# Window attention: scores on four 64x64 tiles into two banks, weighted sums with loaded values in column tiles, norms transposed back into their own bank

## The chip, the cores and the metric

The kernel runs on one core of one Trainium2 chip, as one program in which the instructions of every engine are written out by hand. TensorE is called PE here, VectorE DVE, ScalarE ACT, GpSimd POOL and SyncE SP. The metric is the time of one execution in device microseconds (us). Three executions of the kernel before took 2562.41 us (median), 2558.15 and 2567.25 us.

## The reference

The input `x` is (8, 128, 64, 64). It goes through a block of window attention and then through a binarized 3x3 convolution with a batch norm.

```python
WIN, HEADS, DOWN, STRIDE = 8, 8, 4, 2            # 64 tokens in a window, 8 heads of 16 channels
def mha(q, k, v, wq, wk, wv, wf, bf):
    qh, kh, vh = (q @ wq), (k @ wk), (v @ wv)    # each split into 8 heads of 16
    attn = softmax(einsum('bqhd,bkhd->bhqk', qh, kh) / sqrt(16))
    return einsum('bhqk,bkhd->bqhd', attn, vh) @ wf + bf

# level 0: self attention in 8x8 windows of x, layernorm; averaged 4x4 -> a 16x16 map
# level 1: the same on the 16x16 map -> kv
# cross:   q = 8x8 windows of level 0; k, v = 8x8 windows of kv, two pixels apart
q = layernorm(level0 + mha(level0_windows, kv_windows, kv_windows, ca_wq, ...))
out = layernorm(q + relu(q @ ffn_w1 + b1) @ ffn_w2 + b2)
y = conv3x3(sign(out), sign(weight)); result = out + batchnorm(y)
```

Each window has, for each of its 8 heads, a 64x64 matrix of scores, its softmax, and a weighted sum of 64 values of 16 channels.

## The kernel before

**Units and pairs.** An image is cut into 8 strips of 8 rows; a strip has 8 windows of 64 tokens, taken two at a time: four pairs. The unit of work is one strip of self attention (64 `self` units), one strip of cross attention with the feed-forward part and a strip of the convolution (64 `cross` units), or the 16x16 map of an image (8 `low` units of two pairs). That makes 528 pairs. The first 16 self units run alone; then self and cross units take turns, 96 units of 4 pairs each, with a low unit put in here and there; the last 16 cross units run alone. After them comes a tail that applies the batch norm and adds (DMA, ACT and DVE; PE has no work there).

**What sets the order.** `stages_in_order` gives every stage of a unit an offset in pairs (the tables `SELF`, `CROSS`, `LOW`, `LAST_CONV`), sorts all stages of all units by unit start plus offset, and every engine issues its own stages in that one order. Pair `k` of a unit has `rough` at `k - 1.95`, `scores` at `k - 1.0`, `exp` at `k - 0.98`, `prob_lo` at `k - 0.96` and `weigh` at `k + 0.5`. So, in the time of one pair, PE meets in this order: the scores of pair n, the rough scores of pair n+1, whatever has an offset whose fraction lies between 0.05 and 0.5, the weighted sum of pair n-1, and whatever has a fraction from 0.5 to 1. I call the two places for other work the **first gap** (rough to weigh) and the **second gap** (weigh to the next scores and rough). DVE has the reduction of the rough scores (`maxima`) at the `rough` place and `normalise` at the `weigh` place.

**One pair.** `rough_scores` (L591) makes the 8 heads x 2 windows of 64x64 scores into `ps_max`, window w on partitions 64w to 64w+63. DVE reduces them (L897, `negmax`). `scores` (L601) makes them again, transposed, into `ps_s`, and L607 subtracts the maxima by 16 small matmuls. ACT takes the exponential twice (L769 in f32, L770 in f16) and POOL the difference (L1055). `weigh` (L620) is 12 matmuls with the probabilities loaded (128x128) and 68 columns of values streamed, into `ps_o`; column 32 of a block of values is one, so that the sum of the probabilities comes out beside them. `normalise` takes the reciprocal of the 8 sums a token (L904) and multiplies (L909, twice) into `onorm`, which has tokens on its partitions.

**One unit.** `turn` (L633) transposes `onorm` on PE into `ps_t`, ACT copies it to `oT` (L781, four pieces), and `project` (L652) multiplies by `wf` into `ps_y`, onto which `resid` (L639, L641) had put the input and the bias. `stats` (L919, L924), `rstd` on POOL and `apply` (L932) normalise; `spread` (L660) transposes back into `ps_t`; ACT applies gain and shift (L801). A cross unit then has `h0` to `h3` (L672), `f0` to `f3` (L683), a second norm (L938, L943, L951), `out` (L691) into `ps_t`, and `conv` (L702). The projections of q, k and v go through `ps_proj` (L535, L560); v is split into two f16 parts (L748 on ACT, L880 on DVE) and moved into the windowed layout `vb` by a DMA (`move_v`). For cross units the values come from DRAM (`fetch_v`).

Each of `ps_proj, ps_hid, ps_max, ps_s, ps_o, ps_t, ps_y, ps_y2` is one bank of PSUM. `rough` waits for the reduction of the pair before (`s_neg`), `weigh` for the normalise of the pair before (`s_on`): the two chains don't touch one another.

## Time and profile before

| | |
|---|---|
| three executions | 2562.41 us median (2558.15 to 2567.25) |
| the profiled execution | 2557.35 us, of which the span of the trace is 2555.5 us |
| PE busy | 2160.4 us (85%) |
| DVE busy | 1596.3 us (62%) |
| ACT busy | 1368.0 us (54%) |
| POOL busy | 943.8 us (37%) |
| mean granted PE clock | 0.937 of full speed |
| tail after the last pair | about 165 us without PE work |

The page counts an engine as busy from the start to the end of an instruction's row. On PE these rows overlap heavily, since a row includes the time in which results run out of the array; the distance between the starts of two blocks of matmuls is what a block costs PE. The chain that ended last is followed back from the last instruction, always to what released it.

### The profile page before, as it was taken

The page shows a single profiled execution, that of the slowest core. Times are in us where ns is not written, and L with a number is a line of the kernel's source. Part 1 is how long each engine was busy: PE and PEld are TensorE (multiplying, and loading weights), DVE is VectorE, ACT ScalarE, POOL GpSimd, SP SyncE. Part 2 cuts the span into 40 slices and gives each one's busy share as a digit, 9 for nine tenths or more (in the row PEclk, how much of TensorE's full clock was granted, in tenths as well). Part 3 has the DMA queues.
Part 4 walks back from the last instruction along what each step waited for, and adds up shares of the span by engine and source line. Part 5 has one row for each costly group of instructions (what it writes and reads, how often), then busy time and mean ns, then how long its engine had stood idle before and what let it go on. Part 6 is the DMA issues. An engine that isn't in the chain of part 4 may idle for free.

```text
span 2555.5 us, 93135 instructions
## 1 busy us (share of the span) xinstructions
PE 2160.4 (85%) x39704; PEld 1729.7 (68%) x39704; DVE 1596.3 (62%) x5098; ACT 1368.0 (54%) x2531; POOL 943.8 (37%) x1080
## 2 busy tenths in 40 slices
PE   6987889997999979998899979999799989898700
PEld 4776767775777757776677757777677767676400
DVE  4886766676666757776576656676567655555332
ACT  3664555664556646665455645565456544555332
POOL 3443443443344334434344433443344433333100
PEclk9999999999999989998899989999899999999955
DMA  6775655554555545554455545555455544432177
GB/s 183 210 196 162 190 147 160 168 164 125 155 165 166 154 122 165 164 158 137 132 166 151 166 120 151 160 168 143 129 162 162 161 120 118 122 113 85 44 238 261
DMA packets 335102, 393.57 MB, mean 154 GB/s; under 512 B 40033, under 2 KB 239458, under 8 KB 334690
## 3 DMA queue, kind: packets, MB, share of 16 engines
q1 hardware_dynamic: 333842, 386.62, 52.5%
q8 instruction: 315, 5.16, 0.9%
q10 hardware_dynamic: 848, 0.99, 0.1%
q14 instruction: 97, 0.79, 0.1%
HBM read 208.29 MB, written 160.27 MB: 144 GB/s over the span
## 4 chain that ended last, share of the span: by engine, by line
PE 58%; DVE 28%; DMA 4%; ACT 4%; issue 4%; POOL 1%; SPq 0%; POOLq 0%; DVEq 0%; ACTq 0%
PE ps_hid L672 9%; PE ps_y L683 9%; PE ps_proj L535 6%; PE ps_o L620 6%; DVE onorm L909 5%; PE ps_s L601 4%; PE ps_hid L702 3%; PE ps_s L607 3%; PE ps_t L633 3%; DVE negmax L897 3%; DVE xn L951 3%; PE ps_max L591 3%; PE ps_y L652 2%; PE ps_y L639 2%; DVE xn L932 2%
## 5 line engine op out<-in xcount | busy, mean ns | idle before, releaser
L1055 POOL TENSOR_TENSOR prob_lo<-prob,prob_hi 128x512 f16<-128x512 f32 x528 | 611.1, 1157 | 913.9 <-ACT prob_hi L770 913.9
L769 ACT ACTIVATE prob<-ps_s 128x512 f32<-128x512 f32 x528 | 313.6, 594 | 399.8 <-PE ps_s L607 394.1
L897 DVE TENSOR_REDUCE negmax<-ps_max 128x8 bf16<-128x512 f32 x528 | 360.4, 683 | 119.8 <-PE ps_max L591 115.5
L904 DVE RECIPROCAL rden<-ps_o 128x8 f32<-128x8 f32 x528 | 107.1, 203 | 518.7 <-PE ps_o L620 517.8
L909 DVE TENSOR_TENSOR onorm<-ps_o,rden 64x128 f32<-64x128 f32 x1056 | 304.9, 289 | 25.5
L770 ACT ACTIVATE prob_hi<-ps_s 128x512 f16<-128x512 f32 x528 | 313.5, 594 | 0.0
L620 PE MATMUL ps_o<-vb,prob_hi 128*128 128x68 f16 x4224 | 293.8, 197 | 3.1 <-DVE onorm L909 2.9
L672 PE MATMUL ps_hid<-xf,w_sb 128*128 128x512 f32 x512 | 286.0, 641 | 3.0 <-ACT yconv L827 2.1
L683 PEld LDWEIGHTS ps_y<-w_sb,hid 128*128 128x128 f32 x2048 | 266.5, 196 | 31.7 <-issue 26.8
L683 PE MATMUL ps_y<-w_sb,hid 128*128 128x128 f32 x2048 | 277.6, 280 | 0.6 <-ACT hid L808 0.6
L620 PEld LDWEIGHTS ps_o<-vb,prob_hi 128*128 128x128 f16 x4224 | 260.7, 100 | 9.7 <-issue 5.4
L620 PE MATMUL ps_o<-vb,prob_lo 128*128 128x68 f16 x2112 | 259.1, 197 | 0.0
L1046 POOL TENSOR_TENSOR vareps<-mv,consts_sb 128x4 f32<-128x4 f32 (+1 forms) x200 | 39.7, 198 | 536.8 <-DVE mv L924 305.2
L601 PE MATMUL ps_s<-qs,ks 64*64 64x64 f16 x8448 | 235.2, 197 | 1.5 <-ACT prob_hi L770 1.5
L601 PEld LDWEIGHTS ps_s<-qs,ks 64*64 64x64 f16 x8448 | 176.2, 110 | 81.8 <-issue 55.1
L607 PE MATMUL ps_s<-identb,negmax 64*64 64x64 bf16 x8448 | 225.0, 195 | 3.8 <-DVE negmax L897 3.8
L591 PE MATMUL ps_max<-ks,qs 64*64 64x64 f16 x8448 | 225.3, 195 | 0.2 <-issue 0.2
L620 PEld LDWEIGHTS ps_o<-vb,prob_lo 128*128 128x128 f16 x2112 | 204.5, 100 | 23.5 <-issue 4.1
L781 ACT ACTIVATE oT<-ps_t 64x256 f32<-64x256 f32 (+1 forms) x544 | 201.6, 371 | 14.5 <-PE ps_t L633 7.8
L808 ACT ACTIVATE hid<-ps_hid,columns_sb 128x512 f32<-128x512 f32 x256 | 175.9, 687 | 57.9 <-PE ps_hid L672 55.8
L1049 POOL TENSOR_TENSOR rstd<-vareps,consts_sb 128x4 f32<-128x4 f32 (+1 forms) x200 | 198.8, 994 | 15.7
L932 DVE TENSOR_SCALAR xn<-ps_y,mv,rstd 128x128 f32<-128x128 f32 x528 | 180.3, 403 | 27.8 <-POOL rstd L1049 26.8
(106 smaller groups left out, 3554.0 us busy)
## 6 DMA issues: line engine op xcount, KB each, us to landing
k_rows<-k_flat SPq DMA_DIRECT2D x256, 256.0 KB, 3.2
qs<-q_rows SPq DMA_DIRECT2D x512, 128.0 KB, 3.2
ks<-k_rows SPq DMA_DIRECT2D x128, 512.0 KB, 4.9
q_rows<-q_flat SPq DMA_DIRECT2D x128, 256.0 KB, 2.4
vb<-v_flat SPq DMA_DIRECT2D x128, 136.0 KB, 4.2
vb<-values_out SPq DMA_DIRECT2D x128, 136.0 KB, 2.9
xin<-in_x SPq DMA_DIRECT2D x64, 256.0 KB, 3.1
self_out<-xa SPq DMA_DIRECT2D x64, 256.0 KB, 3.6
```

Source lines behind the costliest of these rows:

```text
L591: done = mm(ps_max[r, TOK * h:TOK * h + TOK], qs[u.b][r, h, k, :], ks[u.b][r, h, k, :], start=True, stop=True, skip_group_check=True)
L601: mm(ps_s[r, TOK * h:TOK * h + TOK], ks[u.b][r, h, k, :], qs[u.b][r, h, k, :], start=(h == 0), stop=False, skip_group_check=True)
L607: done = mm(ps_s[r, TOK * h:TOK * h + TOK], negmax[r, pair_no(u, k) % 2, h:h + 1].to_broadcast([64, TOK]), identb[r, r], start=False, stop ...
L620: done = mm(ps_o[:, 2 * VC * j:2 * VC * j + 2 * VC].rearrange("p (w c) -> p w c", w=2), pp[:, pair_no(u, k) % 2, 128 * j:128 * j + 128], v ...
L672: mm(ps_hid[:, :], w1_sb[:, C * b:C * b + C], xf[:, u.no % 2, :], start=True, stop=True, skip_group_check=True).then_inc(s_hid, 1)
L683: done = mm(ps_y2[:, C * p:C * p + C], hid[:, b % 2, C * p:C * p + C], w2_sb[:, b, :], start=False, stop=(b == FB - 1), skip_group_check=True)
L769: activation(prob[:, pair_no(u, k) % 2, :], ps_s[:, :], ACT.Exp)
L770: activation(prob_hi[:, pair_no(u, k) % 2, :], ps_s[:, :], ACT.Exp).then_inc(s_exp, 1)
L897: v.tensor_reduce(negmax[:, pair_no(u, k) % 2, :], ps_max[:, :].rearrange("p (a t) -> p a t", t=TOK), AX.X, ALU.max, negate=True).then_inc ...
L909: done = v.tensor_tensor(onorm[r, u.seq % 2, k, :].rearrange("p (w j d) -> p j w d", w=2, j=4), blocks[r, :, :, DH * h2:DH * h2 + DH], r2[ ...
L932: v.tensor_scalar(xn[:, C * p:C * p + C], ps_y[:, C * p:C * p + C], mv[:, p, 0:1], rstd[:, p:p + 1], ALU.subtract, ALU.mult).then_inc(s_xn, 1)
L1055: g.tensor_tensor(prob_lo[:, i, :], prob[:, i, :], prob_hi[:, i, :], ALU.subtract).then_inc(s_prob, 1)
```

## The change

1. **Scores.** In `rough_scores` and `scores` even heads now write partitions 0 to 63 and odd heads 64 to 127, window 0 into the first and window 1 into the second of two banks (`ps_max` and `ps_s` are two banks each, 256 columns used in each). The 16 matmuls of 64x64 so fall on four row and column positions of the array, where they fell on two. The matmuls that subtract the maxima load a 128-row, 64-column operand.
2. **Weighted sums.** `weigh` now loads values (128 rows x 32 columns) and streams probabilities: 24 matmuls of 64 columns into `ps_o`, and 8 of 128 columns with a loaded block of ones (`vone`) into `ps_sum`, on four column positions. The result has channels on its partitions, and every channel has its own copy of the sum. `ps_o` and `ps_sum` are columns 256 to 511 of the first bank of `ps_max`; hence `max_free`: a rough block waits for the normalise of the weigh block before it, and a weigh block for the reduction of the rough block before it.
3. **Normalise** takes a reciprocal of 128x128 and one product of 128x128, straight into `oT`. `turn`, `turned`, `onorm` and `ps_t` are gone; `project` waits for the last normalise.
4. **Transposes back.** `spread` writes into `ps_y` and `out` into `ps_y2`, over what they were made from. `resid` waits for `s_spread_taken` and `resid2` for `s_out_taken`, where they waited for `s_xn` and `s_xn2`.
5. **Values.** `project_v` is 16 matmuls of 64x64 (f32) into both halves of the partitions, `v_hi` and `v_lo` are two instructions each on 64 partitions and write `vb` directly; `move_v` is gone. `VC` is 32, and the blocks that `fetch_v` brings are zero in half of their channels: 64 x 2048 f16 for each DMA, 64 x 1088 before.
6. All offsets are new.

```diff
-VC = 34
+VC = 2 * DH
...
-SELF = dict(load=-10.6, q=-7.8, q_hi=-7.6, q_lo=-7.45, q_put=-7.3, q_move=-5.7, k=-6.8, k_hi=-6.6, k_lo=-6.45,
-            k_put=-6.4, k_move=-5.1, v=-5.8, v_hi=-5.6, v_lo=-5.45, v_move=-4.3, turn=4.16, turned=4.24, resid=5.2,
...
+SELF = dict(load=-11.6, q=-7.8, q_hi=-7.6, q_lo=-7.45, q_put=-7.3, q_move=-5.7, k=-6.8, k_hi=-6.6, k_lo=-6.45,
+            k_put=-6.4, k_move=-5.1, v=-4.65, v_hi=-4.4, v_lo=-4.2, resid=4.0, project=4.4, stats=4.6, rstd=4.65,
+            apply=5.15, spread=5.86, spread_out=5.96, store=6.4, pool=6.9)
...
+    max_use, use = {}, None
+    for stage, u, what in order:
+        if stage in ("rough", "weigh"):
+            max_use[stage, u.seq, what] = use
+            use = (stage, pair_no(u, what))
...
-        ps_proj, ps_hid, ps_max, ps_s, ps_o, ps_t, ps_y, ps_y2 = (
-            bank(n) for n in ("ps_proj", "ps_hid", "ps_max", "ps_s", "ps_o", "ps_t", "ps_y", "ps_y2"))
+        ps_max, ps_s = two_banks("ps_max"), two_banks("ps_s")
+        ps_proj, ps_hid, ps_y, ps_y2 = (bank(n) for n in ("ps_proj", "ps_hid", "ps_y", "ps_y2"))
+        ps_o, ps_sum = ps_max[:, 0, 256:384], ps_max[:, 0, 384:512]
...
+            def max_free(stage, u, k):
+                if max_use[stage, u.seq, k] is not None:
+                    before, no = max_use[stage, u.seq, k]
+                    pe.wait_ge(s_neg if before == "rough" else s_on, no)
...
             def rough_scores(u, k):
...
-                if pair_no(u, k) > 1:
-                    pe.wait_ge(s_neg, pair_no(u, k) - 1)
+                max_free("rough", u, k)
                 for h in range(HEADS):
+                    to, at = slice(64 * (h % 2), 64 * (h % 2) + 64), TOK * (h // 2)
                     for win in range(2):
                         r = slice(64 * win, 64 * win + 64)
-                        done = mm(ps_max[r, TOK * h:TOK * h + TOK], qs[u.b][r, h, k, :], ks[u.b][r, h, k, :],
+                        done = mm(ps_max[to, win, at:at + TOK], qs[u.b][r, h, k, :], ks[u.b][r, h, k, :],
                                   start=True, stop=True, skip_group_check=True)
...
-                        r = slice(64 * win, 64 * win + 64)
-                        done = mm(ps_s[r, TOK * h:TOK * h + TOK],
-                                  negmax[r, pair_no(u, k) % 2, h:h + 1].to_broadcast([64, TOK]),
-                                  identb[r, r], start=False, stop=True, skip_group_check=True)
+                        n = 4 * win + h // 2
+                        done = mm(ps_s[to, win, at:at + TOK],
+                                  negmax[:, pair_no(u, k) % 2, n:n + 1].to_broadcast([128, TOK]),
+                                  identb[:, to], start=False, stop=True, skip_group_check=True)
...
             def weigh(u, k):
...
                 pe.wait_ge(s_prob, pair_no(u, k))
-                if pair_no(u, k) > 1:
-                    pe.wait_ge(s_on, pair_no(u, k) - 1)
-                for j in range(4):
+                max_free("weigh", u, k)
+                i = pair_no(u, k) % 2
+                for win in range(2):
                     for n, (pp, part) in enumerate(((prob_hi, 0), (prob_lo, 0), (prob_hi, 1))):
-                        done = mm(ps_o[:, 2 * VC * j:2 * VC * j + 2 * VC].rearrange("p (w c) -> p w c", w=2),
-                                  pp[:, pair_no(u, k) % 2, 128 * j:128 * j + 128], vb[u.b][:, :, part, 4 * k + j, :],
-                                  start=(j == 0 and n == 0), stop=(n == 2), skip_group_check=True)
+                        for j in range(HEADS // 2):
+                            at = 256 * win + TOK * j
+                            mm(ps_o[VC * j:VC * j + VC, TOK * win:TOK * win + TOK], vb[u.b][:, part, k, win, j, :],
+                               pp[:, i, at:at + TOK], start=(win == 0 and n == 0), stop=(n == 2),
+                               skip_group_check=True)
+                for n, pp in enumerate((prob_hi, prob_lo)):
+                    for j in range(HEADS // 2):
+                        done = mm(ps_sum[VC * j:VC * j + VC, :].rearrange("p (w t) -> p w t", w=2), vone[:, :],
+                                  pp[:, i, :].rearrange("p (w j t) -> p j w t", w=2, t=TOK)[:, j, :, :],
+                                  start=False, stop=(n == 1), skip_group_check=True)
                 done.then_inc(s_pv, 1)
...
             def attention_residual(u):
                 if before_resid[u.seq] is not None:
-                    pe.wait_ge(s_xn, xn_done[before_resid[u.seq].seq])
+                    pe.wait_ge(s_spread_taken, spread_no["spread", before_resid[u.seq].seq, None])
...
             def project_out(u):
-                pe.wait_ge(s_t_taken, turn_no["turn", u.seq, None])
+                pe.wait_ge(s_on, last_pair(u))
...
-                v.reciprocal(r2, blocks[:, :, :, 32]).then_inc(s_rden, 1)
+                v.reciprocal(rden[:, i, :], ps_sum).then_inc(s_rden, 1)
                 dve.wait_ge(s_rden, pair_no(u, k))
-                for h2 in range(2):
-                    r = slice(64 * h2, 64 * h2 + 64)
-                    done = v.tensor_tensor(
-                        onorm[r, u.seq % 2, k, :].rearrange("p (w j d) -> p j w d", w=2, j=4),
-                        blocks[r, :, :, DH * h2:DH * h2 + DH],
-                        r2[r, :, :].unsqueeze(3).to_broadcast([64, 4, 2, DH]), ALU.mult)
-                done.then_inc(s_on, 1)
+                v.tensor_tensor(oT[:, u.seq % 2, C * k:C * k + C], ps_o, rden[:, i, :], ALU.mult).then_inc(s_on, 1)
```

In the names of the rows below, `[waits ...]` are the semaphores that an instruction waits for. On PE in the middle of the program, before, at the place where a cross unit's q projection stands: `consts_sb,onorm` is the turn, `w_sb,hid` the feed-forward part.

```order
L591 MATMUL ps_max<-ks,qs 64x64 [waits s_neg]
L591 MATMUL ps_max<-ks,qs 64x64 x15
L633 MATMUL ps_t<-consts_sb,onorm 128x128 [waits s_t_taken,s_on]
L633 MATMUL ps_t<-consts_sb,onorm 128x128 x3
L683 MATMUL ps_y<-w_sb,hid 128x128 [waits s_hid_taken]
L683 MATMUL ps_y<-w_sb,hid 128x128 x3
L535 MATMUL ps_proj<-xin,wq_sb 128x256 [waits s_proj_lo,s_xin0]
L535 MATMUL ps_proj<-xin,wq_sb 128x256
L620 MATMUL ps_o<-vb,prob_hi 128x68 [waits s_on,s_prob,s_v_moved0]
```

The same place of the program with the change: between a rough block and the weigh block stand a q projection, both parts of the second residual, a feed-forward part, a hidden block and the output projection of a self unit.

```order
L597 MATMUL ps_max<-ks,qs 64x64 [waits s_on]
L597 MATMUL ps_max<-ks,qs 64x64 x15
L531 MATMUL ps_proj<-xin,wq_sb 128x256 [waits s_proj_lo,s_xin1]
L531 MATMUL ps_proj<-xin,wq_sb 128x256
L647 MATMUL ps_y<-consts_sb,xf 128x128 [waits s_out_taken]
L647 MATMUL ps_y<-consts_sb,xf 128x128 x3
L649 MATMUL ps_y<-brow,ones 128x512
L691 MATMUL ps_y<-w_sb,hid 128x128 [waits s_hid_taken]
L691 MATMUL ps_y<-w_sb,hid 128x128 x3
L680 MATMUL ps_hid<-xf,w_sb 128x512 [waits s_hid_taken]
L660 MATMUL ps_y<-wf_sb,oT 128x128 [waits s_on]
L660 MATMUL ps_y<-wf_sb,oT 128x128 x3
```

The rough block waits for `s_on` where it waited for `s_neg`, and the turn is gone. What stands in the first gap is now unequal from pair to pair: in this pair it is the most, in two of eight pairs nothing.

On DVE, before, around one `normalise` (L904, L909) and the reduction (L897):

```order
L904 RECIPROCAL rden<-ps_o 128x8 [waits s_pv]
L909 TENSOR_TENSOR onorm<-ps_o,rden 64x4x2x16 [waits s_rden]
L909 TENSOR_TENSOR onorm<-ps_o,rden 64x4x2x16
L867 SCALAR_TENSOR_TENSOR q_flat<-ps_proj,q_flat 128x2x256 [waits s_proj_hi]
L938 BN_STATS stats<-ps_y 128x6 [waits s_f]
```

With the change (`ps_max` stands here for `ps_o` and `ps_sum`, which lie in it):

```order
L917 RECIPROCAL rden<-ps_max 128x128 [waits s_pv]
L920 TENSOR_TENSOR oT<-ps_max,rden 128x128 [waits s_rden]
L870 SCALAR_TENSOR_TENSOR q_flat<-ps_proj,q_flat 128x2x256 [waits s_proj_hi]
L965 TENSOR_REDUCE colsum<-xa 128x128 [waits s_pooled,s_spread_taken]
L971 TENSOR_REDUCE low_sum<-colsum 128x32 [waits s_xlow,s_colsum]
```

The reciprocal grew from 8 to 128 elements on each partition, and two products became one.

## Rows read from the trace of the kernel before

**Rows 1.** The page: busy time by engine, and the chain that ended last.

```profile
PE 2160.4 (85%) x39704; PEld 1729.7 (68%) x39704; DVE 1596.3 (62%) x5098; ACT 1368.0 (54%) x2531; POOL 943.8 (37%) x1080
...
PE 58%; DVE 28%; DMA 4%; ACT 4%; issue 4%; POOL 1%; SPq 0%; POOLq 0%; DVEq 0%; ACTq 0%
```

**Rows 2.** Stretches, instructions on `rden` (three a pair): busy, PEclk, DMA share, GB/s.

```profile
40.00:260.00 220.00, 48.51 (x189) 0.98 0.69 192
600.00:1800.00 1200.00, 208.43 (x801) 0.95 0.53 151
2040.00:2380.00 340.00, 47.12 (x181) 0.96 0.37 107
```

**Rows 3.** Who waited for whom: us in total, times, longest.

```profile
DVE rden L904 <- PE ps_o L620: 517.8, 285, 4.3
...
PE ps_t L633 <- DVE onorm L909: 9.3, 31, 1.1
...
PE ps_o L620 <- DVE onorm L909: 2.9, 12, 1.0
```

**Rows 4.** Groups by line and shape: busy us, mean ns | idle before, releaser.

```profile
L897 DVE TENSOR_REDUCE negmax<-ps_max 128x8 bf16<-128x512 f32 x528 | 360.4, 683 | 119.8 <-PE ps_max L591 115.5
...
L909 DVE TENSOR_TENSOR onorm<-ps_o,rden 64x128 f32<-64x128 f32 x1056 | 304.9, 289 | 25.5
...
L781 ACT ACTIVATE oT<-ps_t 64x256 f32<-64x256 f32 x512 | 193.0, 377 | 11.4 <-PE ps_t L633 4.9
...
L904 DVE RECIPROCAL rden<-ps_o 128x8 f32<-128x8 f32 x528 | 107.1, 203 | 518.7 <-PE ps_o L620 517.8
```

**Rows 5.** PE in order of time at full clock: start, length, instructions.

```profile
1247.52 0.60 PE L639 MATMUL ps_y<-consts_sb,xin 128*128 128x128 f32 x4
...
1248.17 0.60 PE L639 MATMUL ps_y<-consts_sb,xf 128*128 128x128 f32 x4
...
1249.71 0.19 PE L620 MATMUL ps_o<-vb,prob_hi 128*128 128x68 f16 x1
...
1250.05 0.20 PE L620 MATMUL ps_o<-vb,prob_hi 128*128 128x68 f16 x1
1250.18 0.44 PE L601 MATMUL ps_s<-qs,ks 64*64 64x64 f16 x16
1250.45 0.42 PE L607 MATMUL ps_s<-identb,negmax 64*64 64x64 bf16 x16
...
1250.70 0.42 PE L591 MATMUL ps_max<-ks,qs 64*64 64x64 f16 x16
1251.05 1.12 PE L672 MATMUL ps_hid<-xf,w_sb 128*128 128x512 f32 x2
1252.02 1.05 PE L652 MATMUL ps_y<-wf_sb,oT 128*128 128x128 f32 x8
...
1258.96 0.63 PE L633 MATMUL ps_t<-consts_sb,onorm 128*128 128x128 f32 x4
1259.43 1.06 PE L683 MATMUL ps_y<-w_sb,hid 128*128 128x128 f32 x8
1260.32 1.03 PE L535 MATMUL ps_proj<-xin,wq_sb 128*128 128x256 f32 x4
...
1270.25 2.12 PE L702 MATMUL ps_hid<-smap,convs 128*128 128x512 bf16 x9
1272.31 0.44 PE L601 MATMUL ps_s<-qs,ks 64*64 64x64 f16 x16
```

**Rows 6.** DVE in order of time, the same stretch.

```profile
1250.29 0.21 DVE L904 RECIPROCAL rden<-ps_o 128x8 f32<-128x8 f32 x1 [2.35 <-PE ps_o L620]
...
1253.11 0.89 DVE L919 BATCH_NORM_STATS2 stats<-ps_y 128x6 f32<-128x128 f32 x4 [1.25 <-PE ps_y L652]
...
1255.88 1.37 DVE L932 TENSOR_SCALAR xn<-ps_y,mv,rstd 128x128 f32<-128x128 f32 x4 [0.68 <-POOL rstd L1049]
...
1258.92 0.69 DVE L897 TENSOR_REDUCE negmax<-ps_max 128x8 bf16<-128x512 f32 x1 [0.33 <-PE ps_max L591]
```

262 lines of the change are left out of this document (123 added, 139 removed).

## The prediction

> **What bounds the kernel now.** I read the busy shares first [rows 1]: PE 85%, DVE 62%, ACT 54%, POOL 37%, so PE is the fullest engine, but the chain that ended last is PE for only 58% and DVE for 28%. A kernel bound by PE alone would show PE throughout. Then the pace [rows 2]: with three `rden` instructions a pair, 63 pairs take 220 us where self units run alone (3.49 us a pair), 267 take 1200 us in the middle (4.49), 60.3 take 340 us where cross units run alone (5.64). The clock there is 0.95 to 0.98, so it stands at its lower level (1.2 GHz) for a few per cent only. Third, the waits [rows 3]: DVE waited 517.8 us for weighted sums, which is slack of DVE; a weigh block waited 2.9 us for the normalise before it, the turn 9.3 us. Last, a stretch in order of time [rows 5, 6] shows the period: scores, maxima, rough scores, other work, weighted sum. At full clock a block costs PE the distance to the next start: scores 0.27, maxima 0.25, rough 0.35, weigh 0.47, together 1.34 us a pair.
>
> **What PE loses and gains in a pair.** The 16 matmuls of a score block take 0.25 us on two positions of the array [rows 5]. On four positions they take 0.13 if these really work at once; that is worth 2 x 0.12. The maxima block keeps two positions: 0.25. The weigh block has 12 matmuls in 0.34 + 0.03 us. The new one streams 24 x 64 and 8 x 128 columns in four column positions; at the 0.03 us that 68 columns take now this is 40 times 0.03 over four, 0.29 us (at two positions' spacing of 15 ns each, 0.48). So 0.3 us are saved. Against this stands a change of shape: inside a weigh block starts are 0.03 apart, from its last one to the scores 0.13, and rough to the next work is 0.35 where maxima to rough is 0.25 [rows 5]. A change of tile shape costs 0.09 to 0.1. There are two a pair now; with 64x64, 128x64, 64x64, 128x128, 128x32 and 128x128 there are four to six. They cost 0.2 to 0.4 us. PE gains nothing in a pair. The Trainium skill (TensorEngine Tiling (Array Packing), Key Properties) says that changing the tiling mode drains the engine; that speaks against this change, and the trace's 0.1 us agrees.
>
> In a unit PE loses the turn, 0.47 us [rows 5], 136 times: 64 us less. ACT loses four copies of 377 ns, 1.5 us a unit [rows 4]. The values' projection keeps its column passes on two positions at best, and gets two changes of shape; ACT and DVE each get one more instruction of some 0.6 us in a self unit. The DMA that moved values goes; the fetched block grows from 1088 to 2048 elements a row. DMA engines are at 0.53 [rows 2], and the fetch stands over four pairs ahead of its use: nothing.
>
> **Normalise.** Products of 128 elements take 289 ns, a reduction of 512 elements 683 ns [rows 4]: 1.03 ns an element and a fixed 150 to 157 ns. The reciprocal takes 203 ns for 8 elements. Either its fixed part is 195 ns, and 128 elements take 0.33 us; or its fixed part is that of the others and each element takes (203 - 152)/8 = 6.4 ns, and 128 take 0.97 us. No other DVE row here has a fixed part as large as 195, so I take 0.97 and keep 0.33 as the other end. With the product (0.35 with its hand-over) normalise is then 1.32 us (or 0.68); now it is 0.203 and two products, 0.8 us and the hand-over [rows 4]. The Trainium skill (VectorE: DVE Perf Modes, Walkthrough: the 8-slice pipeline in each mode) describes the reciprocal as an iterative division with a repeat count of 8; taken as 8 cycles an element it would lie near the slow end, but the page gives no duration.
>
> **The shared bank.** This is the largest term. With the change rough waits for the normalise of the weigh ahead of it, and weigh for the reduction of the rough ahead of it; what stands behind either on PE's queue waits too. One turn of this loop is: hand-over 0.05, weigh 0.30 at the clock of the middle, 0.23 until DVE starts (0.58 from first start to normalise now, less 0.34), normalise R + 0.35, hand-over 0.05, rough 0.13, 0.20 until DVE starts (the row of 0.42 less 0.25, and 0.03), reduction 0.71. That is 2.02 + R: 2.99 us, or 2.35. Other work comes on top as far as it doesn't fit in the gaps: in the first gap PE has about 0.8 us while DVE reduces, DVE 0.68 while PE weighs; in the second DVE has 0.48, PE R + 0.62 less the scores and maxima with their changes of shape (0.6 to 0.75).
>
> The offsets repeat every eight pairs of the middle. Prices: q and k 0.86, v, project and each feed-forward part 0.89, a residual 0.65, a hidden block 0.97, conv 2.06 [rows 5], spread and out 0.44, a little under the turn; on DVE an apply 1.3 [rows 6], and as estimates from 1.03 ns an element and 0.09 us fixed (0.15 less the overlap of neighbouring rows) a split of q, k or v 0.62, four statistics with their aggregates 1.2 (0.89 for the statistics alone [rows 6]), pooling 0.9. By the offsets the PE work in first and second gap is 1.75/2.05, 0.86/0.44, 0/0.97, 1.85/0.65, 4.25/0, 1.85/1.33, 0.89/0, 0/1.10; DVE's is 0/1.84, 1.92/0.62, 0/0, 0/1.23, 0/1.84, 1.30/0, 1.22/2.20, 0/0. The eight turns then take 5.4, 4.4, 3.1, 4.9, 7.2, 3.6, 5.2 and 3.3 us, 37.1 in all. An example: the fifth has 4.25 us of PE in its first gap, 3.5 more than the gap holds, and then 1.84 of DVE in the second, which the rough block waits out. With R = 0.33 the sum is 34.9.
>
> The same walk over the old order, where the two chains are apart, gives 31.4, and the trace has 8 x 4.49 = 35.9. The missing 4.5 us are the low units' own stages and waits from stage to stage. The kernel with the change has more idle time in which these can vanish; between none and all of it stays, and I take half, having no row that decides. So the middle goes from 35.9 to 37.1 + 2.25: 3.45 us more, in 50 such groups (400 pairs) 172 us. Self units alone: 3.26 by the walk against 3.49 measured before; 3.87 + 0.12 after, times 64: +32. Cross units alone: 4.92 against 5.64; 5.04 + 0.36 after, -0.24 times 64: -15. Sum +189. Against the profiled execution's 2557 (span 2555.5 and 2 around it) this is 2746; the median of the runs shown is 5 us above that one, so I say **2750 us**. With none of the missing part it is 2603, with all of it 2889. The tail without PE stays as it is.
>
> **The rivals.**
>
> *Fast reciprocal.* R is 0.33, the loop still costs. The same sum gives +62 in the middle, 0 and -26 at the ends: 2593, up to 2737 with all of the missing part. For it: a streaming engine at one element a cycle, as all the other rows show. Against it: 203 ns.
>
> *The other side: faster.* R is 0.33 and the missing 4.5 us were mostly the chain that the change removes: last normalise, turn, four copies on ACT, project, where the project stands waiting in PE's queue. Then nothing comes on top of the walk: 34.9 against 35.9 in the middle (-50), -8 and -49 at the ends, 2450. It decides from R + 2.02 being well under the PE work of a pair. For it: the copies are 193 us of ACT [rows 4], in a chain that PE's next work has to fit around. Against it: the turn waited for its normalise only 9.3 us in all [rows 3], and the pair that has no filler still pays the loop.
>
> *Slow reciprocal, all stage waits absorbed:* 2603.
>
> *The change doesn't do what it says:* four positions don't work at once. Score blocks stay at 0.25 and weigh goes to 0.48: some 0.26 us a pair more, 528 times, 2890. Against it: two positions do work at once now, since 16 matmuls of 64 columns start within 0.25 us.
>
> **How the numbers follow.** Forecast (slow reciprocal, about half of the waits) 0.48; slow reciprocal with the waits absorbed 0.10; fast reciprocal with the loop's cost 0.22; faster 0.15; no concurrency 0.05. Time: 2750. The range leaves out most of the last case's upper end and the lowest part of the faster one: 2490 to 2880. A measurement tells 0.3% (8 us) from no change. Faster: 0.15 and a tail of the fast-reciprocal case, 0.18. Same: 0.06, from the cases at 2593 and 2603. Slower: 0.76.
>
> **What would show it.** The row of the new reciprocal: about 970 ns, or about 330. The starts of the 16 matmuls of a score block: 0.13 us from first to last, or 0.25. New PE waits of rough blocks for the product on DVE and of weigh blocks for `negmax`, hundreds of us together; before, weigh has 2.9 us for normalise [rows 3]. DVE's wait for weighted sums should shrink if the reciprocal is slow. The pace in the middle should be near 4.9 us a pair, about 4.0 where self units run alone, 5.4 in the cross end. PE's busy share falls to some 75%, and the granted clock with it. I am wrong if rough and weigh hardly wait, that is, if DVE is through before PE comes back, or if the stage waits were most of what the kernel paid before.

## The result and the profile after

The changed kernel takes 3198.06 us (median of four executions, 3197.53 to 3198.79), the one before 2562.06 us (median of four, 2558.15 to 2567.25). The ratio is 1.2495, 95% interval 1.2473 to 1.2517: **636 us slower**. The prediction had the direction and missed the size: 2750 was forecast, 2880 was the end of its range. The profiled execution took 3198.45 us, span 3196.4.

The page of the kernel after: busy time by engine, the granted clock in 40 slices, the chain that ended last.

```profile
PE 2351.6 (74%) x51368; PEld 1678.8 (53%) x51368; DVE 1885.1 (59%) x4690; ACT 1230.0 (38%) x2107; POOL 941.4 (29%) x1078
...
PEclk9776779888788887888878888798878888999965
...
PE 50%; DVE 33%; ACT 4%; POOL 4%; issue 4%; DMA 3%; SPq 0%; DVEq 0%; POOLq 0%; ACTq 0%
```

No engine is nearly full, and all four are less full than before [rows 1]. PE and DVE share the chain: this is a kernel that waits. The mean granted clock fell from 0.937 to 0.842. PE's busy time rose by 191 us although the turn is gone. Its instructions run longer at the lower clock, as the 512 matmuls of the hidden blocks show, which the change leaves alone (before, then after):

```profile
L672 PE MATMUL ps_hid<-xf,w_sb 128*128 128x512 f32 x512 | 286.0, 641 | 3.0 <-ACT yconv L827 2.1
```

```profile
L680 PE MATMUL ps_hid<-xf,w_sb 128*128 128x512 f32 x512 | 322.3, 715 | 7.4 <-ACT yconv L830 5.8
```

Who waited for whom, after (us in total, times, longest):

```profile
PE ps_max L635 <- DVE negmax L907: 242.5, 198, 4.5
PE ps_max L597 <- DVE oT L920: 153.5, 181, 1.5
PE ps_y L668 <- DVE xn L939: 113.1, 98, 2.0
PE ps_proj L531 <- DVE vb L886: 69.8, 55, 3.0
...
DVE rden L917 <- PE ps_max L640: 636.7, 332, 4.7
DVE negmax L907 <- PE ps_max L597: 341.1, 230, 4.8
DVE xn L939 <- POOL rstd L1056: 102.7, 122, 1.5
```

L635 is the weigh block, L597 the rough block, L668 the spread. The first two rows are the shared bank: 396 us, where the kernel before has 2.9 us [rows 3]. The next two were not forecast: the spread waits for the apply (10.3 us before, the row below), and a projection waits for the values' split on DVE. Over all rows PE waits 717 us, and 262 before. These 455 us and the 191 us of longer busy time make 646, and the span grew by 641. Both engines wait for each other: DVE too waits longer, 637 us for weighted sums (517.8 in [rows 3]) and 341 for rough scores (115.5 in [rows 4]). The spread's wait before:

```profile
PE ps_t L660 <- DVE xn L932: 10.3, 15, 1.2
```

Three groups by line and shape, after (busy us, mean ns | idle before, releaser), beside [rows 4]:

```profile
L917 DVE RECIPROCAL rden<-ps_max 128x128 f32<-128x128 f32 x528 | 502.4, 952 | 636.8 <-PE ps_max L640 636.7
L907 DVE TENSOR_REDUCE negmax<-ps_max 128x8 bf16<-128x512 f32 x528 | 360.7, 683 | 344.4 <-PE ps_max L597 341.1
L920 DVE TENSOR_TENSOR oT<-ps_max,rden 128x128 f32<-128x128 f32 x528 | 153.9, 291 | 18.2
```

The reciprocal of 128 columns takes 952 ns, the one of 8 columns 203 ns.

The pace, read from the reciprocals (one a pair) in three stretches of after; columns are stretch, length, busy and count, PEclk, DMA share, GB/s:

```profile
40.00:300.00 260.00, 49.28 (x52) 0.75 0.42 119
700.00:2100.00 1400.00, 229.31 (x241) 0.85 0.41 118
2600.00:3000.00 400.00, 67.37 (x71) 0.94 0.46 130
```

That is 5.00 us a pair where self units run alone, 5.81 in the middle, 5.63 where cross units run alone. Before, it was 3.49, 4.49 and 5.64 [rows 2]. The cross end lost nothing; the loss is in the first two.

Two pieces of the middle of after in order of time, PE, DVE and POOL (start, length, instructions, idle before and releaser):

```profile
1505.48 0.32 PE L609 MATMUL ps_s<-qs,ks 64*64 64x64 f16 x16
...
1505.73 0.44 PE L616 MATMUL ps_s<-identb,negmax 128*64 128x64 bf16 x16
...
1506.41 0.93 DVE L917 RECIPROCAL rden<-ps_max 128x128 f32<-128x128 f32 x1
...
1507.37 0.29 DVE L920 TENSOR_TENSOR oT<-ps_max,rden 128x128 f32<-128x128 f32 x1
1507.58 0.68 DVE L965 TENSOR_REDUCE colsum<-xa 128x128 f32<-128x512 f32 x1
...
1507.71 0.32 PE L597 MATMUL ps_max<-ks,qs 64*64 64x64 f16 x16 [1.54 <-DVE oT L920]
...
1508.49 1.36 DVE L958 TENSOR_SCALAR xn<-ps_y,mv,rstd 128x128 f32<-128x128 f32 x4
1509.77 0.68 DVE L907 TENSOR_REDUCE negmax<-ps_max 128x8 bf16<-128x512 f32 x1
...
1510.60 0.24 PE L635 MATMUL ps_max<-prob_hi,vb 128*32 128x64 f16 x4 [2.56 <-DVE negmax L907]
...
1520.44 1.01 POOL L1056 TENSOR_TENSOR rstd<-vareps,consts_sb 128x4 f32<-128x4 f32 x1
...
1521.55 1.37 DVE L939 TENSOR_SCALAR xn<-ps_y,mv,rstd 128x128 f32<-128x128 f32 x4 [0.90 <-POOL rstd L1056]
...
1522.97 0.66 PE L668 MATMUL ps_y<-consts_sb,xn 128*128 128x128 f32 x4 [1.64 <-DVE xn L939]
1523.43 0.94 DVE L917 RECIPROCAL rden<-ps_max 128x128 f32<-128x128 f32 x1
...
1524.85 0.43 PE L597 MATMUL ps_max<-ks,qs 64*64 64x64 f16 x16 [0.51 <-DVE oT L920]
```

The first piece is the loop of the shared bank. The rough block waits for reciprocal and product (1.54 us). Its scores are in the bank at about 1508.0, but DVE has 2.3 us of pooling and apply queued, takes the maxima at 1509.77, and the weigh block waits until 1510.60. In the second piece DVE stands still 0.90 us for a root on POOL. The spread waits for the apply. A weigh block that ended at 1521.3 gets its reciprocal only at 1523.43, behind the apply and a statistics step of the convolution (0.68 us), and the next rough block waits for that.

### The profile page after: what moved, and what is told of

Read it like the earlier page. It is cut to its first block, busy times and chain, and to the rows that moved or that the text cites. A ratio compares the mean times of both kernels' runs of the same rounds, so it can differ in the third digit from the quotient of the medians.

```text
span 3196.4 us, 115085 instructions
## 1 busy us (share of the span) xinstructions
PE 2351.6 (74%) x51368; PEld 1678.8 (53%) x51368; DVE 1885.1 (59%) x4690; ACT 1230.0 (38%) x2107; POOL 941.4 (29%) x1078
## 4 chain that ended last, share of the span: by engine, by line
PE 50%; DVE 33%; ACT 4%; POOL 4%; issue 4%; DMA 3%; SPq 0%; DVEq 0%; POOLq 0%; ACTq 0%
DVE rden L917 8%; PE ps_hid L680 7%; PE ps_proj L531 6%; PE ps_y L691 5%; DVE xn L939 4%; PE ps_max L635 4%; PE ps_y L660 4%; POOL rstd L1056 4%; PE ps_s L616 3%; PE ps_proj L559 3%; PE ps_y L647 3%; DVE negmax L907 3%; PE ps_max L597 3%; DVE stats L926 3%; DVE xn L958 3%
## 5 line engine op out<-in xcount | busy, mean ns | idle before, releaser
L917 DVE RECIPROCAL rden<-ps_max 128x128 f32<-128x128 f32 x528 | 502.4, 952 | 636.8 <-PE ps_max L640 636.7
L635 PE MATMUL ps_max<-prob_hi,vb 128*32 128x64 f16 x8448 | 213.8, 208 | 242.6 <-DVE negmax L907 242.5
L635 PEld LDWEIGHTS ps_max<-prob_hi,vb 128*32 128x32 f16 x8448 | 149.0, 104 | 406.9 <-issue 306.7
L597 PE MATMUL ps_max<-ks,qs 64*64 64x64 f16 x8448 | 185.2, 211 | 153.9 <-DVE oT L920 153.5
L616 PE MATMUL ps_s<-identb,negmax 128*64 128x64 bf16 x8448 | 260.6, 210 | 1.4 <-DVE negmax L907 1.4
L939 DVE TENSOR_SCALAR xn<-ps_y,mv,rstd 128x128 f32<-128x128 f32 x528 | 180.8, 404 | 102.7 <-POOL rstd L1056 102.7
L609 PEld LDWEIGHTS ps_s<-qs,ks 64*64 64x64 f16 x8448 | 122.3, 118 | 204.0 <-issue 189.8
L597 PEld LDWEIGHTS ps_max<-ks,qs 64*64 64x64 f16 x8448 | 125.6, 118 | 194.5 <-DVE oT L920 151.1
L616 PEld LDWEIGHTS ps_s<-identb,negmax 128*64 128x64 bf16 x8448 | 198.6, 120 | 26.1 <-DVE negmax L907 1.6
L531 PE MATMUL ps_proj<-xin,wq_sb 128*128 128x256 f32 x512 | 149.7, 417 | 80.9 <-DVE vb L886 50.7
L609 PE MATMUL ps_s<-qs,ks 64*64 64x64 f16 x8448 | 183.8, 210 | 0.0
L668 PE MATMUL ps_y<-consts_sb,xn 128*128 128x128 f32 x528 | 95.7, 307 | 113.2 <-DVE xn L939 113.1
```

What stands on the lines that cost most here:

```text
L531: done = mm(ps_proj[:, win * n:(win + 1) * n], w, src[:, win, :, :], start=True, stop=True, skip_group_check=True)
L597: done = mm(ps_max[to, win, at:at + TOK], qs[u.b][r, h, k, :], ks[u.b][r, h, k, :], start=True, stop=True, skip_group_check=True)
L616: done = mm(ps_s[to, win, at:at + TOK], negmax[:, pair_no(u, k) % 2, n:n + 1].to_broadcast([128, TOK]), identb[:, to], start=False, stop=T ...
L635: mm(ps_o[VC * j:VC * j + VC, TOK * win:TOK * win + TOK], vb[u.b][:, part, k, win, j, :], pp[:, i, at:at + TOK], start=(win == 0 and n == ...
L917: v.reciprocal(rden[:, i, :], ps_sum).then_inc(s_rden, 1)
```

## The experiments

Kernel 1 is the kernel of experiment 1, and so on; each was timed once, in its profiled execution. The kernel before, run beside each group of them, took 2561.9 to 2572.1 us, so a difference of 10 us between two of them says little. Differences are against after (3198) unless another kernel is named. Behind each result stands where it fell in what was expected.

**1. The weighted sums in a bank of their own.** `ps_s` shrinks to one bank (the scores in two halves, the subtraction between them), and `ps_o` and `ps_sum` get the bank that this frees. Offsets and reciprocal stay. The halves are 8 matmuls each on two positions of the array, so this layout has a cost of its own, in the text below an estimated 110 us in all.

```diff
-        ps_max, ps_s = two_banks("ps_max"), two_banks("ps_s")
-        ps_o, ps_sum = ps_max[:, 0, 256:384], ps_max[:, 0, 384:512]
+        ps_max = two_banks("ps_max")
+        ps_o, ps_sum = ps_w[:, 0:128], ps_w[:, 128:256]
...
-                max_free("rough", u, k)
+                if pair_no(u, k) > 1:
+                    pe.wait_ge(s_neg, pair_no(u, k) - 1)
```

> The kernel with the change, but the weighted sums and their sums of probabilities have a bank of their own: rough waits for the reduction before it, weigh for the normalise before it, as before the change. The bank comes from the scores, which go into one bank in two halves on two array positions each (eight matmuls, the maxima, eight matmuls). That costs PE 0.12 us and one more change of tile shape (0.1 us) a pair, some 110 us in all at full clock. Theory A (the shared bank's loop is the main loss): the two new waits (rough for the product 153 us, weigh for the reduction 242 us) vanish, PE has less idle time and the granted clock rises from 0.842 to 0.90 or more; 2700 to 2850 us. Theory B (the loss is the longer reciprocal and the new order of stages, whatever bank is used): the waits move to other blocks, the clock stays, 3050 us or more.

Measured: 3028.9 us, 169 less, between the two ranges. Waits, own bank:

```profile
PE ps_y L676 <- DVE xn L947: 197.5, 106, 4.1
...
PE ps_y L706 <- DVE xn L966: 67.5, 48, 4.2
PE ps_w L643 <- DVE oT L928: 61.9, 81, 1.6
```

The 396 us of waits for the shared bank are gone save 62 for the normalise of the pair before, but the spread's wait for the apply grew from 113 to 197, and the wait of `out` for the second apply from 6 to 68. What moving out of the shared bank gains is 169 us of the 636, net of what the halves cost: behind its waits stood others.

**2. A reciprocal of 8 of the 128 columns**, in the changed kernel (the other columns are a constant, so part of the computation is left out).

```diff
-                v.reciprocal(rden[:, i, :], ps_sum).then_inc(s_rden, 1)
+                v.reciprocal(rden[:, i, 0:8], ps_sum[:, 0:8]).then_inc(s_rden, 1)
```

> The kernel with the change, but the reciprocal is taken of 8 of the 128 columns only (the other factors are a constant; this part of the computation is left out, to time the rest). DVE's row shrinks from 952 to about 200 ns, 0.75 us a pair, 397 us in all. Theory A (rough waits for normalise in a loop that the reciprocal is part of): most pairs get 0.5 to 0.75 us shorter and the clock rises a little, 2800 to 2930 us. Theory B (the loop matters only where PE has no other work; stage waits and the clock decide): under 0.25 us a pair, 3070 us or more.

Measured: 2973.5 us, 225 less, for 396 us of DVE time; that too lies between the two ranges. The rough block's wait fell from 153.5 to 31.8 us; the weigh block's didn't:

```profile
PE ps_max L635 <- DVE negmax L907: 256.4, 199, 4.5
...
PE ps_max L597 <- DVE oT L920: 31.8, 42, 0.8
```

**3. ACT copies the sums out of the bank**, so that the rough block waits for one copy (`s_oc`) and not for reciprocal and product.

```diff
-                    pe.wait_ge(s_neg if before == "rough" else s_on, no)
+                    pe.wait_ge(s_neg if before == "rough" else s_oc, no)
...
+                activation(osum[:, pair_no(u, k) % 2, :], ps_max[:, 0, 256:512], ACT.Identity).then_inc(s_oc, 1)
```

> The kernel with the change, but ACT copies both halves of the shared bank (256 columns) to SBUF behind each weigh block, the rough block waits for this copy in place of the product, and DVE normalises from the copy. All of the work stays, and ACT gets about 0.38 us a pair. Theory A: the loop gets shorter by about 0.9 us (reciprocal and product, 1.25 us, leave it; the copy enters), PE's wait for the product goes, and the wait for negmax stays; 2900 to 3000 us. Theory B (DVE's total work is what counts): within 2% of 3198 us.

Measured: 3349.1 us, 151 more. Both theories are wrong. Waits:

```profile
PE ps_max L637 <- DVE negmax L915: 399.4, 228, 5.7
...
DVE rden L925 <- ACT osum L794: 821.7, 345, 6.3
...
ACT osum L794 <- PE ps_max L642: 659.2, 444, 5.7
```

The rough block's wait is off the list, but DVE gets its sums later (637 to 822 us of waiting), and the weigh block's wait for the maxima grew from 243 to 399. The copy is seldom late by ACT's queue: in 444 of 528 pairs ACT stood and waited for the weigh block. What comes on top is the copy itself, 0.38 us a pair ahead of the normalise. DVE still issues the normalise ahead of the next maxima, so the copy puts off both, and the loop from one weigh block to the next got longer and not shorter. That is read from these rows and not tested apart.

**4. PE filled with matmuls that nobody reads**, 13 of 512 columns a unit, in 13 self units of the opening.

```diff
+            def extra(u, count):
+                if u.kind == "self" and 4 <= u.at < 56:
+                    for _ in range(count):
+                        mm(ps_hid[:, :], identb[:, :], convs[:, 0:4, :].rearrange("p a b -> p (a b)"),
```

> The kernel with the change, with 13 idle-filling matmuls of 512 columns a unit (bf16, into the bank of the hidden blocks, which nothing uses there; their results are never read) in 13 self units of the opening stretch only. They stand where PE waits. Theory C (a lower granted clock, due to PE's idle time, makes all of PE's own work longer): between 60 and 250 us the granted clock rises from 0.75 to over 0.9 and the pace goes from 5.05 us a pair to 4.6 or less, some 20 to 30 us off the whole. If the clock doesn't matter there, the pace stays at 5.05 or gets worse by what doesn't fit in the gaps (up to 0.3 us a pair).

Measured: 3183.1 us, 15 less, where 20 to 30 were expected. The stretch 60 to 240 us in after (first fence) and here (second), reciprocals only:

```profile
60.00:240.00 180.00, 34.40 (x36) 0.75 0.42 120
```

```profile
60.00:240.00 180.00, 36.22 (x38) 0.91 0.44 126
```

More work on PE, and the pace went from 5.00 to 4.74 us a pair (4.6 or less was expected) as the granted clock rose. The count of 36 or 38 is coarse, but 15 us in the 52 pairs of these 13 units are 0.29 a pair, much the same. So the clock is part of the cost, some 0.26 us of the 1.5 that a pair lost there. It is a consequence: with PE waiting, a larger part of the time is at 1.2 GHz, which lengthens the loop that makes it wait.

**5. Before's offsets, all the rest of the change kept** (shared bank, wide reciprocal). The values' projection keeps its new place; the second residual stands half a pair later than before (9.95), and the low units' chain 0.7 later, from 3.7 on.

```diff
-            k_put=-6.4, k_move=-5.1, v=-4.65, v_hi=-4.4, v_lo=-4.2, resid=4.0, project=4.4, stats=4.6, rstd=4.65,
-            apply=5.15, spread=5.86, spread_out=5.96, store=6.4, pool=6.9)
+            k_put=-6.4, k_move=-5.1, v=-4.65, v_hi=-4.4, v_lo=-4.2, resid=5.2,
+            project=6.2, stats=6.5, rstd=6.55, apply=6.9, spread=7.56, spread_out=7.66, store=8.0, pool=8.6)
```

> The kernel with the change and its shared bank, with the offsets of the kernel before for residual, project, statistics, apply, spread, feed-forward and convolution (second residual 9.95 in place of 9.45, because it now waits for the copy out of its bank; the low units' chain starts at 3.7); only the stages of v keep their new places. If the new offsets cost much (statistics, reciprocal root on POOL and apply stand within 0.6 of a pair, so that DVE waits for POOL with normalise behind it, and one gap holds 4.25 us of PE work), this runs in 2850 to 3050 us. If the offsets are suited to the new waits, 3198 us or more.

Measured: 3005.7 us, 192 less and in the range: the new offsets cost as much as the bank. Waits:

```profile
PE ps_max L597 <- DVE oT L920: 204.6, 297, 1.7
PE ps_max L635 <- DVE negmax L907: 130.0, 126, 2.8
...
PE ps_y L668 <- DVE xn L939: 16.8, 10, 2.4
```

The spread's wait went from 113 to 17 us, and DVE's wait of `xn` (L939) for the root from 103 to 13.

**6. Own bank and before's offsets together.**

> The bank of its own for the weighted sums (3029 us with the new offsets) together with the offsets of before as in shared_old_order. What is left of the change against the kernel before is then the reciprocal of 128 columns (0.75 us more of DVE a pair), the changes of tile shape, and no turn. Theory A+B (bank and offsets together are the loss, the reciprocal has room in DVE's 35% of idle time): 2600 to 2720 us. Theory R (the reciprocal itself is the loss, because it stands in DVE's queue ahead of the work PE waits for): 2850 us or more.

Measured: 2821.2 us, 377 less, between the two ranges. 169 and 192 are 361: the two add up. Seen from here, the shared bank costs 185 us (kernel 5) and the new offsets 208 (kernel 1). So the new offsets cost as much with a bank of its own as with the shared one.

**7. The same with the reciprocal of 8 columns** (computation left out as in 2).

> As own_bank_old_order, with the reciprocal of 8 of the 128 columns only (this part of the computation is left out). It prices the reciprocal where nothing else of the change stands in its way. Theory A+B: 50 to 120 us less than own_bank_old_order. Theory R: 250 us less or more, and near 2500 us, under the kernel before, since the turn and its four copies are gone.

Measured: 2664.4 us, 157 less than kernel 6, again between the two theories, and 100 over the kernel before, not under it.

**8. The wide reciprocal alone, in the kernel before.** It takes 16 columns of each block of sums where it took one, 128 elements; the result is the same.

```diff
-                v.reciprocal(r2, blocks[:, :, :, 32]).then_inc(s_rden, 1)
+                v.reciprocal(rden[:, pair_no(u, k) % 2, :, :, :], blocks[:, :, :, 17:33]).then_inc(s_rden, 1)
```

> The kernel before with one thing changed: its reciprocal takes 16 columns of each block of sums, 128 on each partition in place of 8, and the product uses one of them as before. The result is the same; DVE's row should be 950 ns as in the kernel with the change, 0.75 us more a pair, 395 us in all. Theory R: 2562 plus 200 us or more. Theory A+B: plus 100 us or less.

Measured: 2826.5 us, 262 more than before, as theory R has it; granted clock 0.912, and the reciprocal takes 954 ns. The turn's wait for normalise grew from 9.3 us [rows 3] to

```profile
PE ps_t L633 <- DVE onorm L909: 84.6, 105, 1.7
```

One instruction that is 0.75 us longer on DVE, an engine that had 38% idle time, costs 0.5 us a pair with the order, the banks and PE's work untouched. The idle time was not where the instruction needed it.

**9. One tile shape for scores and maxima.** The maxima are subtracted with 64x64 tiles, behind the next rough block, so that three blocks follow in one shape. Once with the shared bank, once in kernel 6.

```diff
+            row.append((u.at + k - 0.94, "minus", u, k))
...
-                                   negmax[:, pair_no(u, k) % 2, n:n + 1].to_broadcast([128, TOK]),
-                                   identb[:, to], start=False, stop=True, skip_group_check=True)
+                                   negmax[to, pair_no(u, k) % 2, n:n + 1].to_broadcast([64, TOK]),
+                                   identb[to, to], start=False, stop=True, skip_group_check=True)
```

> The kernel with the change, with the maxima subtracted by 64x64 tiles (the 64 rows that matter, on two array positions) behind the next rough block in place of 128x64 tiles ahead of it. The matmuls and columns stay the same; two of four to six changes of tile shape a pair go, at 0.095 us each 100 us of PE's time. If they are on the path as PE's other work is, 3198 less 70 to 110 us. If PE's idle time hides them, within 30 us of 3198.

> own_bank_old_order (2821 us) with the same edit: maxima on 64x64 tiles behind the rough block. PE is nearer to being the bound here, so all of the 100 us should show: 2700 to 2750 us. If it is DVE's reciprocal alone that holds this version above the kernel before, 2790 us or more.

Measured: 3210.2 us with the shared bank, 12 more, within the 30 of PE's idle time hiding the changes of shape. The subtraction now stands behind the rough block's wait, which reads 254.5 us for 153.5, while the weigh block's fell from 243 to 181; all PE waits together rose from 717 to 764. No gain from the saved changes can be seen. In kernel 6's setting, 2785.2 us, 36 less, where all of the 100 us were expected to show, and near the 2790 of the other theory.

**10. The same edit where the reciprocal is short** (kernel 7 with it, computation left out as there).

> Own bank, before's offsets, a reciprocal of 8 of the 128 columns (part of the computation is left out), and the maxima taken off on 64x64 tiles behind the next rough block. What is left of the change is the new scores and weighted sums, the transposed order of the values, and the new place of the values' projection. It was 2664.4 without the last edit, 100 us over the kernel before. Theory E (the changes of tile shape are a third of these 100, as the 36 us with the wide reciprocal say): 2625 to 2640, clock about 0.93. Theory F (with DVE's reciprocal out of the way PE is the bound and every change of shape counts: 2 x 0.1 us x 528): 2560 to 2590. If they are hidden: 2655 to 2670.

Measured: 2637.4 us, 27 less than kernel 7: theory E's range holds and F falls. The edit also moves the subtraction, so the 27 are not the shapes alone. Even with short normalises and a bank of its own, these changes of shape are a small part. The Trainium skill (TensorEngine Tiling (Array Packing), Key Properties) says that changing the mode drains the engine. The trace agrees with some 0.1 us each: scores (L609) to subtraction (L616) is 0.25 us in the first piece in order of time above, where 16 matmuls on four positions take 0.12. But a saving of one or two changes a pair would be 50 to 100 us if all of it were on the path, and 12 more, 36 less and 27 less were measured: so most of it seems to lie in time in which PE waits anyway.

**11. Apply and spread later**, with shared bank and new offsets kept. The low units' steps from residual to spread move by 0.1 to 0.45 with them: with these left in place the waits of the order close a circle, and the kernel would never end.

```diff
-            apply=5.15, spread=5.86, spread_out=5.96, store=6.4, pool=6.9)
+            apply=5.6, spread=6.4, spread_out=6.44, store=6.6, pool=6.9)
```

> The changed kernel, shared bank and new offsets kept, but the apply step of self and cross units stands 0.45 of a pair later (5.6 for 5.15) and the spread 0.54 later (6.4 for 5.86), so that the root on GpSimd has more time before DVE's apply waits for it; the low unit's steps from residual to spread move by 0.1 to 0.45 to fit between. Theory C (the chain statistics, root, apply, spread is what the new offsets cost, some 190 of the 192 us that the old ones save): DVE's wait of xn for rstd (102.7 us) and PE's wait of the spread for xn (113.1 us) go nearly away, and the time falls by 100 to 190 us, to 3010 to 3100. Theory D (the new offsets cost because filler work now stands in the gaps of the shared bank's loop, and the chain's waits only lie where the loop would wait anyway): those two rows shrink, but the waits of rough and weigh grow by as much, and the time stays within 30 us of 3198.

Measured: 3127.3 us, 71 less, short of the 100 to 190 of theory C. Waits:

```profile
PE ps_max L635 <- DVE negmax L907: 178.2, 141, 3.2
PE ps_max L597 <- DVE oT L920: 173.1, 185, 1.5
...
PE ps_y L668 <- DVE xn L939: 77.4, 59, 2.1
...
DVE xn L939 <- POOL rstd L1056: 8.6, 8, 2.4
```

DVE's wait of `xn` (L939) for the root fell from 103 to 9 us, the spread's from 113 to 77, and the weigh block's from 243 to 178, while the rough block's rose from 154 to 173. So the chain statistics, root, apply, spread is real, and is a third of what the offsets cost. Theory C is right in kind and too large; theory D falls.

**12. Where the other 120 us of the offsets lie.** Before's offsets for the feed-forward and convolution steps alone, and the same with the later apply.

```diff
-             h0=6.6, relu0=6.8, h1=7.4, relu1=7.6, resid2=8.25, f0=8.27, h2=8.35, relu2=8.5, f1=9.1, h3=9.15,
-             relu3=9.3, f2=9.6, f3=10.1, stats2=10.35, rstd2=10.4, apply2=10.95, out=11.85, out_take=11.95,
+             h0=8.2, relu0=8.4, h1=9.2, relu1=9.4, resid2=9.95, f0=9.97, h2=10.2, relu2=10.4,
+             f1=10.3, h3=11.2, relu3=11.4, f2=11.3, f3=12.2, stats2=12.6, rstd2=12.65, apply2=13.4, out=13.8,
```

> The changed kernel with the shared bank and the new offsets for the attention's own steps (residual to spread, loads, values), but before's offsets for the feed-forward and convolution steps of cross units. All of before's offsets saved 192 us, a later apply and spread 71. Theory G (the rest, some 120 us, lies in the feed-forward part: new offsets put two or three parts of it beside each other, so that PE has 4 us of filler in one gap of the loop and nothing in the next): 3198 - 120, so 3060 to 3100. Theory H (the rest is in the residual and projection of self units, which come 1.2 to 1.8 pairs earlier and stand close behind the last normalise): 3180 to 3200.

> Both edits: the later apply and spread (alone -71) and before's offsets for the feed-forward steps. Under theory G the two together recover most of the 192 us: 3005 to 3040. Under theory H they recover no more than the later apply alone: 3110 to 3130.

Measured: 3411.2 us, 213 more, and with the later apply 3146.0, 19 more than kernel 11. Both times are outside the ranges of both theories, the second by 16 us. Waits of the first:

```profile
PE ps_y L698 <- DVE xn L958: 174.7, 64, 4.5
...
DVE negmax L907 <- PE ps_max L597: 578.2, 276, 6.3
```

`out` waits 2.7 us in each of the 64 cross units, DVE waits for rough scores 578 us where it waited 341, and the later apply takes 265 us off this kernel where it took 71 off after. Offsets can't be priced one step at a time: they repeat every eight pairs, and what a step costs depends on what shares its gap. Which steps hold the other 120 us stays open.

## Why the size was wrong

From the kernel before to the changed one, each step a pair of runs. Kernels 7 and 10 leave out part of the computation. Kernels 6, 7 and 10 have the halves of experiment 1, so the bank's step is net of them. The price of a step depends on what stands around it: the reciprocal is 157 us here, 225 in after (2) and 262 in the kernel before (8); the bank is 185 here and 169 with the new offsets; the offsets are 192 here and 208 with a bank of their own.

| from, to | us |
|---|---|
| before, to new scores, weighted sums and values with a short reciprocal, one shape, own bank, before's offsets (10) | 2562 to 2637: +75 |
| the subtraction in its own shape (7) | +27 |
| the reciprocal of 128 columns (6) | +157 |
| the shared bank (5) | +185 |
| the new offsets (after) | +192 |

**Right.** The reciprocal's price (0.97 for 952 ns) and so the choice against the fast one; four positions working at once; the price of a change of shape; the two new waits of the shared bank; a PE busy share of some 75% (74); the pace of the cross end (5.4, measured 5.6). PE gaining nothing in a pair agrees with kernel 10, which is 75 us slower without wide reciprocal, shared bank and new offsets, though it has a cost of its own (see below).

**Wrong: the turns of the loop.** The forecast for eight pairs of the middle was 37.1 us and half of the missing 4.5, together 39.4; the trace has 8 x 5.81 = 46.5. That is 7.1 us in each of 50 groups, 357 us. Self units alone add 1.0 us in each of 64 pairs. Together that is 421 of the 448 us by which 2750 was too low. The turns of the walk add up to 37.1; it is their input that failed. Two steps of the sum did.

The first is "The missing 4.5 us are the low units' own stages and waits from stage to stage", of which "between none and all of it stays, and I take half". The walk filled the two gaps with the lengths of other work and let each piece start when its gap came. It had no terms for a piece that isn't ready: the apply that waits for a root of 1.01 us on POOL, the spread behind the apply, and the maxima or the reciprocal that are queued on DVE behind them. I argued that the new idle time would hide such waits. It did the opposite: the middle is 4.9 us in eight pairs above even "all of it stays" (37.1 and 4.5 are 41.6). The second of the two pieces in order of time shows one such wait, and kernel 11 puts 71 us to it. The walk had priced the whole change at 5.7 us in eight pairs (31.4 to 37.1), 285 us in 50 groups; the middle grew by 10.6 (35.9 to 46.5). Bank, reciprocal and offsets cost 157 to 262 us each (table). That the two chains now meet in one bank doesn't explain the excess, though it is where the forecast looked: the new offsets cost 208 us without the shared bank (kernel 6 to kernel 1), and the reciprocal costs 262 us where the chains are apart (kernel 8). How the excess splits over the eight turns stays open.

The second is the clock. The sum kept the clock of before: the middle fell from 0.95 to 0.85, the opening from 0.98 to 0.75. The prediction said that the clock would fall, and didn't put it into the sum. Its size, as an estimate: kernel 10 and after have the same number of matmuls, and PE is busy 2130 us at a mean clock of 0.921 in the one, 2352 us at 0.842 in the other; the ratio of the clocks alone makes 2330 of 2130. So most of the 222 us between them is clock. Not all of it lies on the path: in kernel 4's stretch a clock of 0.91 for 0.75 gave back 0.26 us of 1.5 a pair.

**Wrong: a sign that I named.** DVE's wait for weighted sums was to shrink if the reciprocal is slow. It grew from 518 to 637 us. For the reciprocal by itself the sign held: in kernel 8 that wait is 486.5 us, in kernel 6 it is 413. The shared bank (523 in kernel 5) and the new offsets (526 in kernel 1) each add 110, and together they make the 637.

**Of the rivals**, none was what happened. The fast reciprocal and the absorbed waits (2593 and 2603) fall with the 952 ns and with the grown waits, the faster one with both, and the one without concurrency (2890) is nearest in number and wrong in kind. What was missing is an upper end beyond "all of the 4.5 us stays" (2889): the range ended near there, though no row bounded the waits from above. Kernel 8 would have been the warning: by itself the wide reciprocal costs 262 us in the old kernel, more than the 189 that the sum had for the whole change.

**Open.** The 75 us of kernel 10 (65, against the kernel before in its own group, 2572). Its PE rows name candidates, none of them tested by itself:

```profile
PE ps_y L711 <- DVE xn L971: 93.4, 64, 4.2
PE ps_proj L534 <- DVE vb L899: 58.6, 47, 2.9
PE ps_y L681 <- DVE xn L952: 35.4, 27, 2.7
PE ps_y L660 <- ACT smap L838: 26.0, 15, 1.7
```

With a smaller row each, the second and the fourth are 75 us of waits of the projections for the values' split on DVE, and 42 us of residuals and convolutions that wait for ACT's copy of what `out` left in the bank. The first and the third, `out` and spread behind their applies, were 65.6 and 10.3 us in the kernel before:

```profile
PE ps_t L691 <- DVE xn L951: 65.6, 49, 4.4
```

Against them stand the turn, forecast at 64 us saved, and the residuals' own waits for applies (53.5 us before). And kernels 1, 6, 7 and 10 still carry the halves of experiment 1, which the change doesn't have. In kernel 10 the 8 matmuls of one half lie in

```profile
1001.10 0.31 PE L610 MATMUL ps_s<-qs,ks 64*64 64x64 f16 x8
```

where 16 on four positions lie in 0.32. Two halves so cost PE some 0.12 us a pair more, an estimated 63 us in all if all of it were on the path. The new scores, weighted sums and values by themselves may therefore cost little; no run shows them without the halves, the wide reciprocal and the shared bank.

## What to carry to other kernels

Don't price a longer instruction by the idle share of its engine. In this kernel, where every engine issues in one fixed order, 38% of idle time hid a third of 0.75 us a pair (262 us of 396 came through). Before two chains are put into one bank, write down the loop that the two waits close, and count in it everything that the slower engine has queued between its two steps, with its own waits, not only its lengths. Give a new order of steps a price of its own: here it cost as much as the bank, whichever bank was used. And make the sum again with the lower clock that the longer waits bring.

## What the hardware showed

- A reciprocal on DVE took 952 ns for 128 columns and 203 ns for 8, which is 6.2 ns a column, where products and reductions take 1.03. A copy of the same sum in each of 16 channels is therefore dear to invert.
- 16 matmuls of 64x64x64 on four positions lie in a row of 0.32 us, of which one is 0.19 to 0.21: some 0.12 from the first start to the last. On two positions the row is 0.44, so some 0.24. A change of shape costs about 0.1 us.
- Matmuls without any use, put into PE's idle time, made the useful ones faster: granted clock 0.75 to 0.91, pace 5.00 to 4.74 us a pair, 15 us off the whole.
